# Gated cross-attention with a feed-forward part: keys and probabilities are transposed by DMA, and the output projection adds up per head group

## What is computed

```python
q = rmsnorm((layernorm(x) @ Wq).reshape(B, Sq, H, D), gq)      # 32, 100, 16, 128
k = rmsnorm((ctx @ Wk).reshape(B, Skv, H, D), gk)              # 32, 361, 16, 128
v = (ctx @ Wv).reshape(B, Skv, H, D)
attn = softmax(einsum('bqhd,bkhd->bhqk', q, k) / sqrt(D))
out = einsum('bhqk,bkhd->bqhd', attn, v).reshape(B, Sq, H * D) @ Wo
x = x + tanh(g_xattn[0]) * out
x = x + tanh(g_ffn[0]) * down(silu(gate(layernorm(x))) * up(layernorm(x)))   # ternary weights, 8-bit activations
```

## Time and profile before

| | us |
|---|---|
| median of 3 runs | 2822.2 (2820.04 to 2822.61) |
| the profiled execution's own time | 2822.88 |
| its span, first to last instruction | 2821.1 |
| TensorE busy | 2586.8 (92%) |
| VectorE busy | 2078.7 (74%) |
| ScalarE busy | 1757.5 (62%) |
| GpSimd busy | 744.0 (26%) |

### The profile page before, as it was taken

One profiled execution on the slowest core, in us unless ns is written; L12 is line 12 of the kernel. 1 busy time (PEld: TensorE's weight loads), 2 busy tenths in 40 slices (PEclk: granted clock), 3 DMA queues, 4 the chain that ended last, 5 costly groups with the idle time before them and its releaser, 6 DMA issues. The chain is left out here.

```text
span 2821.1 us, 60152 instructions
## 1 busy us (share of the span) xinstructions
PE 2586.8 (92%) x19714; PEld 1918.6 (68%) x19866; DVE 2078.7 (74%) x5039; ACT 1757.5 (62%) x4314; POOL 744.0 (26%) x1215
## 2 busy tenths in 40 slices
PE   3799999999999999999999999999999999479998
PEld 2577777777777778677777777777777787344443
DVE  5785868686868686777868686868686868259997
ACT  4675757575757576666757575757575757364443
POOL 3232333232322323232323232323233332000000
PEclk8899999999999999999999999999999999789999
DMA  5101010101010000000010001010101000414444
GB/s 181 38 1 30 2 30 1 30 1 30 2 30 1 11 21 2 30 2 30 2 30 1 30 2 30 2 30 2 30 2 30 1 13 1 166 50 112 112 112 101
DMA packets 96011, 93.84 MB, mean 33 GB/s; under 512 B 56208, under 2 KB 67760, under 8 KB 95152
## 3 DMA queue, kind: packets, MB, share of 16 engines
q1 hardware_dynamic: 95664, 89.44, 10.8%
HBM read 63.21 MB, written 13.11 MB: 27 GB/s over the span
## 5 line engine op out<-in xcount | busy, mean ns | idle before, releaser
L498 ACT ACTIVATE ksq<-keys_ps 128x512 f32<-128x512 f32 (+1 forms) x384 | 229.1, 597 | 516.3 <-PE keys_ps L25 510.6
L868 POOL TENSOR_SCALAR kvar<-kss 128x4 f32<-128x4 f32 (+1 forms) x384 | 79.5, 207 | 1416.8 <-DVE kss L649 1416.8
L871 POOL TENSOR_TENSOR krs<-kvar,minus_half 128x4 f32<-128x4 f32 (+1 forms) x384 | 390.1, 1016 | 32.0
L514 ACT ACTIVATE prob<-score_ps,nbias,qrs 100x361 f32<-100x361 f32 x512 | 336.1, 656 | 43.6 <-DVE nbias L681 43.1
L676 DVE TENSOR_REDUCE nmax<-score_ps 100x1 f32<-100x361 f32 x512 | 270.9, 529 | 104.8 <-PE score_ps L25 99.8
L522 ACT ACTIVATE prob<-prob,rden 100x361 f32<-100x361 f32 x512 | 317.8, 621 | 0.9 <-DVE rden L687 0.9
L657 DVE TENSOR_TENSOR khat<-keys_ps,krs 128x512 f32<-128x512 f32 (+1 forms) x384 | 262.7, 684 | 63.2 <-POOL krs L871 63.2
L24 PE MATMUL keys_ps<-wk_lo,ctxT_hi 128*128 128x512 bf16 (+1 forms) x768 | 299.3, 390 | 9.7 <-issue 2.7
L25 PE MATMUL keys_ps<-wk_hi,ctxT_lo 128*128 128x512 bf16 (+1 forms) x768 | 298.2, 388 | 0.0
L649 DVE TENSOR_REDUCE kss<-ksq 128x4 f32<-128x512 f32 (+1 forms) x384 | 262.5, 683 | 14.7 <-ACT ksq L498 7.8
L23 PE MATMUL shared_ps<-xT_hi,wq_hi 128*128 128x200 bf16 x1024 | 255.9, 250 | 15.0 <-DVE wq_lo L643 14.9
(11 more groups left out here) (153 smaller groups left out, 6418.3 us busy)
## 6 DMA issues: line engine op xcount, KB each, us to landing
ctx_raw<-in_ctx SPq DMA_DIRECT2D x32, 256.0 KB, 3.3
xin<-in_x SPq DMA_DIRECT2D x32, 200.0 KB
xres<-in_x SPq DMA_DIRECT2D x32, 200.0 KB
x_rows<-xres SPq DMA_DIRECT2D x32, 200.0 KB
xin<-x_rows SPq DMA_DIRECT2D x25, 256.0 KB, 2.8
xres<-x_rows SPq DMA_DIRECT2D x25, 256.0 KB, 2.7
out<-xres SPq DMA_DIRECT2D x25, 256.0 KB, 2.8
g_raw<-in_L_ffn_w_gate SPq DMA_DIRECT2D x2, 2048.0 KB, 11.0
```

Source lines behind the costliest of these rows:

```text
L498: act.activation(ksq[0:KV[t], k, :], keys_ps[k][0:KV[t], :], ACT.Square).then_inc(ksq_done, 1)
L514: act.activation(prob[:, v % 2, h, 0:SK], score_ps[h % 2][0:SQ, 0:SK], ACT.Exp, bias=nbias[:, col:col + 1], scale=qrs[:, v // 2 % 2, r:r + 1],
L871: pool.tensor_tensor(krs[0:KV[t], k, :], kvar[0:KV[t], k, :], minus_half[0:KV[t], 0:G], ALU.pow).then_inc(krs_done, 1)
```

## The change

1. Keys. `khat` is split where it is made, with context rows on partitions: ScalarE copies the hi half (`keys_hi`), GpSimd subtracts for the lo half (`keys_lo`), both into `ksplit`. SP transposes each tile by one DMA (`turn_keys`: 8 blocks of 128 columns, both halves and four heads) into `kT`, which has a buffer for each batch of the pair. `ksplit` exists once, so the first split of a unit waits for the transposes of the unit before.
2. Probabilities. ScalarE scales and writes the hi half in one step (`probs_hi`), VectorE multiplies and subtracts for the lo half (`probs_lo`), into `psplit`; SP transposes two heads by one DMA (112 rows, 12 blocks). `psplit` exists once, `pT` twice.
3. Projection. `project` runs per head group in every second unit and adds up in two PSUM banks of its own, `y_ps`, which the transposes' two banks have become; a matmul of zeros opens each. `oT` holds one group instead of four.
4. Queries and head outputs go two heads to a bank (400 columns), so their copies, squares and subtractions are half as many and twice as wide. One GpSimd instruction instead of two makes `qrs`.
5. Order. Two units are written together as `two_turns`, and the pair is moved by a unit: the first unit of the first pair, with its mixing, stands ahead of the loop (`first_turn`), together with the queries of two groups. Ahead of the loop, SP issues the last six weight loads behind the key transposes of two units, and the weights of Wv and Wo are split in one piece.

```diff
+            def turn_keys(i, u, t):
+                b, rows = u % 2, -(-KV[t] // 16) * 16
+                sp.wait_ge(k_lo_done, tile(i, u, t) + 1)
...
+                sp.dma_start_transpose(kT[:, b, :, :, t * P:t * P + rows].rearrange("p a h s -> p (a h) s"),
+                                       ksplit[0:rows, t, :, :].rearrange("s a n -> s (a n)")).then_inc(kT_in[b], 16)
+            def turn_probs(i, u, k):
+                b = u % 2
+                sp.wait_ge(p_lo_done, head(i, u, (k + 1) * TWO))
...
+                sp.dma_start_transpose(pT[:, b, k, :, :, :, :].rearrange("p a h t q -> p (a h t) q"),
+                                       psplit[:, k, :, :, :].rearrange("q a h s -> q (a h s)")
+                                       ).then_inc(pT_in[b], 16)
@@ TensorE
-                    last = pe.transpose(turn_ps[h % 2][:, t * P:t * P + KV[t]],
-                                        khat[0:KV[t], u % 2, t, h * D:(h + 1) * D], ident[0:KV[t], 0:KV[t]])
...
-                    last = pe.transpose(turn_ps[h % 2][:, t * SQ:(t + 1) * SQ],
-                                        prob[:, u % 2, h, t * P:(t + 1) * P], ident[0:SQ, 0:SQ])
...
+                if h == 0:
+                    eng.wait_ge(kT_in[b], keys_turned(i, u))
...
+                    eng.wait_ge(pT_in[b], probs_turned(i, u))
...
+                if hg == 0 and m % TWO == 0:
+                    eng.wait_ge(y_added, i * 2 + 1)
+                    pe.matmul(y_ps[m // TWO][:, 0:TWO * QT], zeros[:, :], wk_hi[:, 0, 0:TWO * QT],
+                              start=True, stop=False)
@@ ScalarE
+            def keys_hi(i, u, t):
+                eng.wait_ge(khat_done, tile(i, u, t) + 1)
+                if t == 0 and started(unit(i, u)):
+                    eng.wait_ge(kT_in[1 - u % 2], keys_turned(i, u - 1))
+                copy(ksplit[0:KV[t], t, 0, :], khat[0:KV[t], (u + t) % 2, :]).then_inc(k_hi_done, 1)
...
+            def probs_hi(i, u, h):
+                b = u % 2
+                if h == 0 and started(unit(i, u)):
+                    eng.wait_ge(pT_in[1 - b], probs_turned(i, u - 1))
+                eng.wait_ge(rden_done, head(i, u, h) + 1)
+                act.activation(psplit[0:SQ, h // TWO, 0, h % TWO, 0:SK], prob[:, b, h, :], ACT.Copy,
+                               scale=rden[:, b, h:h + 1]).then_inc(p_hi_done, 1)
@@ VectorE
+            def probs_lo(i, u, h):
+                b = u % 2
+                eng.wait_ge(p_hi_done, head(i, u, h) + 1)
+                dve.scalar_tensor_tensor(out=psplit[0:SQ, h // TWO, 1, h % TWO, 0:SK], in0=prob[:, b, h, :],
+                                         scalar=rden[:, b, h:h + 1], in1=psplit[0:SQ, h // TWO, 0, h % TWO, 0:SK],
+                                         op0=ALU.mult, op1=ALU.subtract).then_inc(p_lo_done, 1)
@@ GpSimd
+            def keys_lo(i, u, t):
+                eng.wait_ge(k_hi_done, tile(i, u, t) + 1)
+                pool.tensor_tensor(ksplit[0:KV[t], t, 1, :], khat[0:KV[t], (u + t) % 2, :], ksplit[0:KV[t], t, 0, :],
+                                   ALU.subtract).then_inc(k_lo_done, 1)
@@ TensorE, order of two units
+                if ku:
+                    keys(i, u + 2, 0), keys(i, u + 2, 1)
+                if qu:
+                    queries(i, u, 0)
...
+                if su:
+                    scores(i, u + 1, 0), scores(i, u + 1, 1)
+                if ku:
+                    keys(i, u + 2, 2)
+                if qu:
+                    queries(i, u, 1)
...
+                if su:
+                    scores(i, u + 1, 2)
+                mixed(i, u, 0)
+                if su:
+                    scores(i, u + 1, 3)
+                if kv:
+                    keys(i, v + 2, 0)
+                mixed(i, u, 1)
...
+                if sv:
+                    scores(i, v + 1, 2)
+                project(i, v, 2), project(i, v, 3)
+                if sv:
+                    scores(i, v + 1, 3)
+                if mv:
+                    mixed(i, v, 0), mixed(i, v, 1)
+                if v == UNITS:
+                    turn_y(i, 0), turn_y(i, 1)
```

More of the change, by code:

```diff
@@ new lines, in shared_uses @@
+        for u in [] if first else range(1, UNITS, 2):
+            v = u + 1
+            if more_queries(u, last):
+                order += [("q", u, 0)]
+            if u == UNITS - 3 and not last:
+                order += [("ctx", 0, 0)]
+            if more_queries(u, last):
+                order += [("q", u, 1)]
+            if u == UNITS - 3 and not last:
+                order += [("ctx", 0, 1)]
+            order += [("m", u, 0), ("m", u, 1)]
+            if u == UNITS - 5 and not last:
+                order += [("x", 0)]
+            if more_queries(u, last):
+                order += [("qss", u)]
+            order += [("o", v, 0), ("o", v, 1)]
+            if u == UNITS - 5 and not last:
+                order += [("x", 1)]
+            if u == UNITS - 3 and not last:
+                order += [("ctx", 1, 0), ("ctx", 1, 1)]
+            if has_mixed(v, last):
+                order += [("m", v, 0), ("m", v, 1)]
@@ new lines, in shared_uses, with has_keys, has_scores, has_mixed @@
+        return order
+    def has_keys(u, last):
+        return u + 2 < UNITS or not last
+    def has_scores(u, last):
+        return u + 1 < UNITS or not last
+    def has_mixed(u, last):
+        return u < UNITS or not last
+    def more_queries(u, last):
+        return u % 2 == 1 and ((u + 3) // 2 < NG or not last)
+    AT_FIRST = {k: n for n, k in enumerate(shared_uses(True, False))}
+    AT_LOOP = {k: n for n, k in enumerate(shared_uses(False, False))}
+    AT_LAST = {k: n for n, k in enumerate(shared_uses(False, True))}
@@ L86, in use, with unit, head, tile @@
         last = isinstance(i, int) and i == PAIRS - 1
[L87 removed]
+        k = (AT_LAST if last else AT_LOOP)[key] + len(AT_FIRST)
         return i * USES + k, k % 2
[L92 to L102 removed]
+    def unit(i, u):
+        return i * UNITS + u
+    def head(i, u, h):
+        return i * (UNITS * G) + (u * G + h)
+    def tile(i, u, t):
+        return i * (UNITS * KVT) + (u * KVT + t)
+    def keys_turned(i, u):
+        return i * (UNITS // 2 * KVT * 16) + (u // 2 + 1) * (KVT * 16)
+    def probs_turned(i, u):
+        return i * (UNITS // 2 * 32) + (u // 2 + 1) * 32
     with ExitStack() as stack:
@@ L150, in attention_block @@
         keys_ps = [bank(f"keys_ps{n}") for n in range(2)]
-        turn_ps = [bank(f"turn_ps{n}") for n in range(2)]
         score_ps = [bank(f"score_ps{n}") for n in range(2)]
         shared_ps = [bank(f"shared_ps{n}") for n in range(2)]
+        y_ps = [bank(f"y_ps{n}") for n in range(YB)]
         pool_passed, dve_passed, sp_passed = sem("pool_passed"), sem("dve_passed"), sem("sp_passed")
@@ L256, in _ @@
+            with sp.Fori(0, PAIRS - 1) as i:
+                for u in range(1, UNITS + 1):
+                    turn(i, u, False)
+            for u in range(1, UNITS + 1):
+                turn(PAIRS - 1, u, True)
             for b in range(2):
@@ L292, in scores @@
[L292 to L308 removed]
+                    eng.wait_ge(exp_done, n - 1)
@@ L481, in _ @@
             eng.wait_ge(w_lo_done, len(pieces))
+            first_turn(-1, UNITS)
             with eng.Fori(0, PAIRS - 1) as i:
-                pair(i, False)
-            pair(PAIRS - 1, True)
+                for u in range(1, UNITS, 2):
+                    two_turns(i, u, False)
+            for u in range(1, UNITS, 2):
+                two_turns(PAIRS - 1, u, True)
         @block.scalar
```

1027 lines of the change are left out of this document (535 added, 492 removed).

## The result

| | before | after |
|---|---|---|
| median, us | 2822.4 (2820.04 to 2822.75, 4 runs) | 2562.5 (2561.42 to 2567.13, 4 runs) |
| ratio, 95% interval | | 0.908 (0.907 to 0.910) |
| a pair in the loop, us | 147.2 | 130.1 |
| the last pair, us | 127 | 105.4 |
| closing adds of pair 1 start at, us | 244.47 | 244.44 |

What follows compares the result with a forecast made beforehand. TensorE was taken to bound the loop. A pair 19.5 us shorter gave −292 over fifteen pairs, with −12 for the last pair and +5 for the startup: 2822.9 − 292 − 12 + 5 = 2524 us, range 2425 to 2670.

Steps and rivals of the forecast that it cites:

- What bounds the kernel: Loop: TensorE is the bound, busy 141.4 of 147.2 us a pair; VectorE comes next.
- the stream's price: TensorE in the loop: removing 192 transposes saves 20 us a pair (18.2 by starts); added matmuls of zeros cost 0.3.
- I let the 3.8 us go.: End of each pair: TensorE's 3.8 us idle before the next scores vanishes, because the new order gives cover.
- The new waits: Joins between engines in the loop: 4 us a pair taken, from 0 up to 14.4 if one per round is exposed.
- The prices on the other engines: Busy time per pair in the loop: VectorE 93 us, ScalarE 79, GpSimd 77; DMA engines under half.
- the lock with GpSimd: VectorE operations with two SBUF inputs and GpSimd operations reading SBUF shut each other out for a whole instruction.
- The ends: Outside the loop: −12 us for the last pair and +5 for the startup, within −3 and +20.
- the moved 10: Some 10 us of the last pair's work moves in front of the loop and cancels in the sum.
- (A): Rival: VectorE and GpSimd take turns in the loop; a pair becomes 140 us, the time 2706; chance 0.17.
- 38 us of room: VectorE in the loop before the change: next after TensorE, busy 109.5 us of a pair, with 38 us of room.
- (B): Rival: DMA transposes don't overlap on the queue; a pair takes 172 us, the time is 3188; chance 0.08.
- (C): Rival: no new waits, a pair is TensorE alone at 122 us; time 2434 or less; chance 0.13.

Runs made afterwards that it cites:

- turns_back: The changed kernel with as many TensorE transposes put back into its stream as the kernel before had for keys and probabilities, their results unused: 2807.4 us.
- unroll3: The changed kernel with three pairs written out per turn of the loop on all engines, in place of one: 2556.2 us.
- before_loop3: The kernel before the change with three pairs written out per turn of the loop on all engines: 2768.5 us.
- startup_order: The changed kernel with the first unit's key transposes issued earlier, its softmax heads interleaved and TensorE's wait for the last weights moved later; loop unchanged: 2551.6 us.
- no_keys_lo: The changed kernel with GpSimd's subtraction for the keys' lower halves cut to one column, so they stay zero: 2531.3 us.
- lo_on_vector: The changed kernel with the subtraction for the keys' lower halves moved from GpSimd to VectorE: 2695.4 us.
- double_keys: The changed kernel with the DMA transposes of each unit's first two key tiles issued twice, the second into a spare buffer: 2609.4 us.

## Why the prediction was right, and where it was off

**What bounds the kernel, and the stream's price.** Right in kind: turns_back shows that the 192 transposes carry nearly the whole gain, at 17.9 us of busy time a pair; the starts of the earlier trace rows gave 18.2. I had added 1.8 for weight loads that stick out; they don't show. With the zeros the forecast had 19.7 us less for TensorE's stream; its busy time fell by 17.8 in the mean pair, 1.9 less.

**"I let the 3.8 us go."** This is the step that failed. It held the idle time at a pair's end for missing cover, which the new order brings. Yet 2.6 of the 3.8 in the earlier trace rows were marked "issue", and that part has nothing to do with cover: it is the loop's return. Over the loop it is 2.8 + 1.2 = 4.0 us a pair before the change, of which the 1.2 went, and 2.6 stand in the changed kernel: 1.4 went where 3.8 were let go, 2.4 us a pair. That it is the return is shown by unroll3 and before_loop3, in which these waits fall from 36.2 us in 14 to 10.8 in 6 and from 38.9 us in 14 to 12.1 in 4. What I also left out is that the clock is lower behind most returns. It is so in both kernels, so it explains what a return costs (5.0 us a pair in the old kernel, 1.8 to 2.4 in the new one) and little of the miss.

**The new waits.** I took 4 us for them. TensorE's idle time outside the return was 2.1 us a pair before and is 4.2 now (6.8 − 2.6), so they cost 2.1. They don't sit where I looked: TensorE waits for the landing of kT 0.4 us in the whole run, while behind the return the waits for qT_lo (33.1 us) and oT_lo (12.3), subtractions on VectorE that free a bank, are the longest of the loop. The term was too large by 1.9.

**The sum.** 1.9 of the stream, 2.4 of the return and −1.9 of the waits make the 2.4 us by which the pair missed (130.1 for 127.7), and 2.4 × 15 = 36 of the 38 us. That two errors of 1.9 cancelled was luck.

**The prices on the other engines.** ScalarE's split 0.63 (0.7 taken), VectorE's 0.62 (0.57), GpSimd's 1.17 (at most 1.34), landings 3.1 and 3.4 us (3 to 4), all within what the rows bounded. VectorE came to 99.8 instead of 93: 4.5 of these are nbias, which the lock with GpSimd stretched, and 1.6 the split's price. The DMA share was 0.56, not 0.45: the loop's 105 GB/s at this share make 188 GB/s for full engines, where 208 was taken.

**The ends.** The last pair lost 21.6 (127.0 to 105.4), the start gained 17.1, each with the moved 10: −12 and +7, against −12 and +5. startup_order shows that 11 us of the start were a matter of order. The range was said to hold waits of 0 to 14.4 us a pair with either end of the startup; waits of 14.4 give 2524 + 15 × 10.4 = 2680 us, outside of its 2670.

**The rivals.** (A), turns between VectorE and GpSimd, did not come: a probability subtraction costs 0.62 us, not 1.6. Its mechanism exists in small, at 0.14 us for each nbias, and no_keys_lo bounds all that GpSimd's subtraction costs at 2.0 us a pair. Too kind was the reading that VectorE has 38 us of room: lo_on_vector shows that at 77% it has none to spare. (B), transposes one after the other, is out, though the changed kernel alone would not show it, since 24 × 3.1 + 16 × 3.4 = 129 us just fit into a pair. double_keys shows it: 56 transposes a pair that landed in 3.2 to 3.7 us would be at least 179 us in a row, and the pair took 133. The Trainium skill's 1309 ns a block (VectorE: DVE Perf Modes, the three transpose paths) would give an estimate of 10.5 us for the eight blocks of one key tile; the row shows 3.1 from issue to landing. (C), 122 us, would have needed the full price of 20 us and no join.

## What to carry to other kernels

Idle time marked "issue" in front of the first instruction of a loop's turn was the return itself in both kernels: count it as fixed, with the slow matmuls that may follow, and don't read it as missing cover. To take it away, write several turns out, but look at every engine's return, the DMA queue's too, since the longer program can cost on one engine what it wins on another. And price work moved to an in-order engine by the waits that others have on it, not by its busy share: 16 us of short subtractions, placed once, on a VectorE that is 77% busy cost 9 us a pair.
